# Tiled attentions of a decoder: row maxima in a ring of single banks, exponentials in halves, the maximum as a row of the query operand

## The reference, cut to what matters

```
scores = q_h @ k_h.T * scale            # 1024 x 1024 for each head
p      = softmax(scores, axis=-1)
out_h  = p @ v_h
y      = concat(out_h) @ Wo
```

## Time and profile before

| what | us |
|---|---|
| median of three runs | 2575.0 |
| the profiled execution, its own time | 2577.73 |
| its span | 2576.1 |
| TensorE matmul busy | 2238.0 (87%) |
| ScalarE busy | 1612.7 (63%) |
| VectorE busy | 985.3 (38%) |
| GpSimd busy | 453.3 (18%) |
| mean granted TensorE clock | 0.927 of 2.4 GHz |

### The profile page before, as it was taken

How to read it: one execution, slowest core, us unless ns; L and a number is a source line. 1 busy time by engine, 2 the same in 40 slices (tenths; PEclk the granted TensorE clock), 3 DMA queues, 4 the chain that set the end, 5 groups by cost and what they waited for, 6 DMA issues and landing times. The chain is left out here.

```text
span 2576.1 us, 30503 instructions
## 1 busy us (share of the span) xinstructions
PE 2238.0 (87%) x12294; PEld 741.9 (29%) x12294; DVE 985.3 (38%) x1557; ACT 1612.7 (63%) x1106; POOL 453.3 (18%) x202
## 2 busy tenths in 40 slices
PE   6999997689979858888799999999999847788797
PEld 2333332244446512222211111111111112222365
DVE  5667763154421366665211011011111146666111
ACT  1999899223322214444499999999999723444433
POOL 0577657200100004555200000000000000000000
PEclk9899999889989969888899999999999967888899
DMA  1000000226641030000100000100000000000010
GB/s 39 9 5 5 5 1 0 107 105 214 208 195 41 0 66 1 1 1 1 41 3 1 25 16 1 31 10 1 1 1 1 2 9 1 1 1 1 20 33 25
DMA packets 28990, 78.95 MB, mean 31 GB/s; under 512 B 3584, under 2 KB 18832, under 8 KB 26784
## 3 DMA queue, kind: packets, MB, share of 16 engines
q1 hardware_dynamic: 15032, 30.91, 4.1%
q0 software_dynamic: 4384, 29.56, 3.3%
q10 hardware_dynamic: 9448, 16.70, 1.8%
HBM read 71.61 MB, written 5.59 MB: 30 GB/s over the span
## 5 line engine op out<-in xcount | busy, mean ns | idle before, releaser
L1613 ACT ACTIVATE crat_E<-banks 128x1536 f32<-128x1536 f32 x544 | 749.4, 1461 | 20.7 <-PE banks L1513 6.8
L1529 PE MATMUL banks<-crat_E,crat_vst 128*32 128x512 f32 x3264 | 436.2, 607 | 0.2 <-ACT crat_E L1613 0.2
L1513 PE MATMUL banks<-crat_Q,mid_arena 52*128 52x512 bf16 x1632 | 329.3, 385 | 21.3 <-ACT crat_E L1613 17.1
L1640 DVE COPY crat_vst<-all_crossV 128x96 f32<-128x96 f32 x136 | 34.2, 252 | 640.7 <-PE banks L1529 640.6
L1276 ACT ACTIVATE rotat_E<-banks 128x2048 f32<-128x2048 f32 x64 | 120.1, 1877 | 178.0 <-PE banks L1167 178.0
L427 POOL TENSOR_TENSOR dist_wsum<-dist_wsum,dist_D 128x1024 f32<-128x1024 f32 x92 | 217.3, 2362 | 8.2
L1276 ACT ACTIVATE lastat_E<-banks 128x2048 f32<-128x2048 f32 x64 | 120.1, 1877 | 146.1 <-PE banks L1167 145.9
L1318 DVE TENSOR_REDUCE rotat_mx<-banks 128x1 f32<-128x512 f32 x256 | 164.9, 686 | 101.4 <-PE banks L1146 101.4
L1318 DVE TENSOR_REDUCE lastat_mx<-banks 128x1 f32<-128x512 f32 x256 | 164.8, 686 | 98.0 <-PE banks L1146 98.0
L345 DVE TENSOR_SCALAR dist_D<-banks,dist_k 128x512 f32<-128x512 f32 x256 | 178.6, 747 | 52.0 <-PE banks L213 52.0
L1513 PEld LDWEIGHTS banks<-crat_Q,mid_arena 52*128 52x128 bf16 x1632 | 60.1, 93 | 442.5 <-ACT crat_E L1613 317.1
(11 more groups left out here) (258 smaller groups left out, 2652.5 us busy)
## 6 DMA issues: line engine op xcount, KB each, us to landing
mlp_M<-in_mask POOLq DMA_DIRECT2D x28, 800.5 KB
mid_arena<-cross_k SPq DMA_DIRECT2D x42, 204.0 KB
moe_W<-in_experts SPq DMA_DIRECT2D x16, 512.0 KB, 3.6
mid_arena<-in_rot_tables ACTq DMA_DIRECT2D x8, 1024.0 KB, 18.1
mlp_C<-in_ctx SPq DMA_DIRECT2D x17, 384.0 KB, 4.4
cross_k<-mlp_kp ACTq DMA_DIRECT2D x17, 288.0 KB, 2.4
mlp_row<-in_mask POOLq DMA_DIRECT2D x1, 3202.0 KB, 12.9
mlp_M<-in_mask POOLq DMA_DIRECT2D x1, 3202.0 KB
```

The source lines that it names most:

```text
L1513: last = pe.matmul(PS[:, 3 * (at % 2) + k, :], K[s:s + ROWS, 2 * (g % 2) + pair, c * P:(c + 1) * P], Q[s:s + ROWS, 2 * g + pair, qh * HALF ...
L1529: last = pe.matmul(PS[32 * j:32 * j + 32, 6 + ps % 2, :], vst[:, (ps * STEPS + c // 3) % 3, c % 3, j, :], E[:, at // 3 % NE, at % 3, :], s ...
L1613: act.activation(flat(E[:, at % NE, :, :]), flat(PS[:, 3 * (at % 2):3 * (at % 2) + 3, :]), ACT.Exp, scale=CROSS_SCALE).then_inc(s_e, 1)
```

## The change

1. In `tiled_attention` a look is one matmul for one head into one bank. The two banks 4 and 5 are a ring: slot `i` waits for the reduce of slot `i - 2`, and the turn and the copy to `F` take a slot of their own. There are 32 looks a pass. They run further ahead: 5 a chunk in pass 0, 4 a chunk from then on, so that a pass's looks end two chunks before it; its turn is at the end of chunk 6 (pass 0: of chunk 7), and VectorE reduces 4 (or 8) looks of the pass after between the maxima and the row.
2. Each exponential is two activations of 128 x 1024. Scores of heads 0 and 1 wait for the first half of the chunk before, those of 2 and 3 for the second.
3. In the plain attention the ones products are gone. Each k tile has a row of ones in a free row of each head's 32, and the query operand `F` (f32 now, made by VectorE from `Q`, a mask and the turned maxima) holds minus the maximum in that row. `mb` is f32 with a copy for each group, its transposes are f32, and scores wait for `F`. The rotary attention keeps the three bf16 parts and the ones products.
4. `rotary_operands` adds on GpSimd and has two `A` buffers. `plain_operands` makes k's product a third time into banks 6 and 7, from which ScalarE casts with a mask as scale.

```diff
# rotary_operands
-                        if i:
-                            dve.wait_ge(s_sum, i)
-                        dve.tensor_tensor(A[:, eo, :], ...
+                        if i >= 2:
+                            dve.wait_ge(s_sum, i - 1)
+                        dve.tensor_tensor(A[:, i % 2, eo, :], ...
-                    dve.tensor_tensor(result(o), A[:, 0, :], A[:, 1, :], ALU.add).then_inc(s_sum, 1)
+                for i, o in enumerate(ORDER):
+                    pool.wait_ge(s_ta, 2 * i + 2)
+                    pool.tensor_tensor(result(o), A[:, i % 2, 0, :], A[:, i % 2, 1, :], ALU.add).then_inc(s_sum, 1)
# plain_operands
-                for o in range(2):
+                for o, at in ((0, 0), (1, 2), (1, 6)):
-                    act.wait_ge(s_k, j + 1)
-                    act.activation(Kb[:, j, :], K[:, j, :], ACT.Copy).then_inc(s_low, 1)
+                    act.activation(Kb[:, j, :], flat(PS[:, 6:8, :]), ACT.Copy, scale=rows[:, 0, j:j + 1]).then_inc(s_low, 1)
-                    dve.tensor_scalar(K[:, j, :], flat(PS[:, 2:4, :]), masks[:, j:j + 1], None, ALU.mult).then_inc(s_k, 1)
+                    dve.tensor_scalar(K[:, j, :], flat(PS[:, 2:4, :]), rows[:, 0, j:j + 1], rows[:, 1, j:j + 1], ALU.mult, ALU.add
# tiled_attention
-    SPREAD = [3, 2, 3, 2, 3, 2, 1, 0]
+    LOOKS = 4 * GROUPS * 2
+    def lag(ps):
+        return 0 if ps in (-1, 0, LAST) else 8 if ps == 1 else 4
+    def look_slot(ps, u):
+        return ps * (LOOKS + 1) + u - (u < lag(ps - 1))
+    def turn_slot(ps):
+        return (ps + 1) * (LOOKS + 1) - 1 + lag(ps)
+    def ahead(ps, c):
+        return min(5 * c if ps == 0 else 8 + LOOKS * ps + 4 * c, LOOKS * LAST)
+    def turned(ps):
+        return (ps - 1, NT - 1 if ps == 1 else NT - 2)
...
-                    pe.wait_ge(s_mt, ps * UNITS + u)
-                    for s in range(2):
-                        r = 32 * (2 * pp + s)
-                        last = pe.matmul(PS[:, MX + s, :], ...
+                def free(i):
+                    if i >= 2:
+                        pe.wait_ge(s_mt, i - 1)
+                    return MX + i % 2
+                    bank = free(look_slot(ps, u))
+                    pe.matmul(PS[:, bank, :], ...
...
                 def scores(ps, c):
-                    if at:
-                        pe.wait_ge(s_e, at)
+                    if c == 0 and not pairs:
+                        pe.wait_ge(s_mt, turn_slot(ps) + 1)
                     for r in range(4):
+                        if at and r % 2 == 0:
+                            pe.wait_ge(s_e, 2 * at - 1 + r // 2)
+                        of = half(Qs(g), ps % 2) if pairs else F[:, ps % 2, :]
+                        last = pe.matmul(PS[:, S + r, :], Ks(g)[32 * r:32 * r + 32, c * P:(c + 1) * P],
+                                         of[32 * r:32 * r + 32, :], start=True, stop=not pairs)
+                        if not pairs and r % 2:
+                            last.then_inc(s_s, 1)
+                    if pairs:
...
+                        for r in range(4):
+                            last = pe.matmul(PS[:, S + r, :], onesb[32 * r:32 * r + 3, :], F[32 * r:32 * r + 3, ps % 2, :],
+                                             start=False, stop=True)
+                            if r % 2:
+                                last.then_inc(s_s, 1)
...
-                    act.activation(flat(E[:, at % NE, :, :]), flat(PS[:, S:S + 4, :]), ACT.Exp, scale=scale).then_inc(s_e, 1)
+                    for i in range(2):
+                        act.wait_ge(s_s, 2 * at + i + 1)
+                        act.activation(flat(E[:, at % NE, 2 * i:2 * i + 2, :]), flat(PS[:, S + 2 * i:S + 2 * i + 2, :]), ACT.Exp,
...
+                for ps in range(PASSES):
+                    for u in range(lag(ps - 1), LOOKS):
+                        reduce(ps, u)
+                    maxima(ps)
+                    for u in range(lag(ps)):
+                        reduce(ps + 1, u)
+                    rows_of(ps)
```

More of the change, by code:

```diff
@@ L1211, in project @@
                         of.then_inc(s_y, 1)
-                pe.wait_ge(s_set, 3)
-                for u in range(UNITS):
-                    look(0, u)
+                pe.wait_ge(s_set, 3 if pairs else 2)
+                for at in range(LOOKS):
+                    look(at)
                 turn(0)
@@ L1219, in _ @@
                         scores(ps, c)
-                        units = range(AHEAD[c], AHEAD[c + 1]) if ps < LAST else range(0)
-                        for u in units[:(len(units) + 1) // 2]:
-                            look(ps + 1, u)
+                        first, end = LOOKS + ahead(ps, c), LOOKS + ahead(ps, c + 1)
+                        middle = (first + end + 1) // 2
+                        for at in range(first, middle):
+                            look(at)
                         if c:
@@ L1226, in _ @@
                             values(ps - 1, NT - 1)
-                        for u in units[(len(units) + 1) // 2:]:
-                            look(ps + 1, u)
+                        for at in range(middle, end):
+                            look(at)
                         if pairs and c == 1 and ps:
@@ L1285, in _ @@
             def _(pool):
-                pool.memset(mb.rearrange("q t w -> q (t w)"), 0.0).then_inc(s_set, 1)
+                of = mb.rearrange("q t w -> q (t w)") if pairs else mb.rearrange("q j t w -> q (j t w)")
+                pool.memset(of, 0.0).then_inc(s_set, 1)
                 def product(ps):
```

141 lines of the change are left out of this document (77 added, 64 removed).

## The result

The changed kernel takes 2487.8 us (four runs, 2483.57 to 2489.26) against 2575.5 for the kernel before (four runs on the same chip): a ratio of 0.9648, with a 95% interval of 0.9621 to 0.9675. Forecast were 2469, in a range of 2435 to 2520. So sign and range hold, and the time is 19 us above the forecast. The profiled execution's span is 2487.4 us, 88.7 less than before, where the terms of the forecast sum to 105.7: 17 us of the gain did not come. (The other 2 us lie in how far a profiled execution stands from the median before and after.)

What follows compares the result with a forecast made beforehand. No engine was full: looks and reduces took turns, and a chain through four score banks was the other limit. Terms summed to -105.7 us from 2577.7, so 2472.0, with the runs' median 2.7 lower: 2469, range 2435 to 2520.

Steps and rivals of the forecast that it cites:

- The forecast case: Whole kernel: the change works as worked out, -105.7 us in sum, to 2469 us; chance 0.68.
- the rotary passes: Rotary attention, passes 1 to 6: 32.5 us a pass against 37.7, -5.2 each, -31.2 in six.
- the passes 0: First pass of each attention: five looks a chunk and a low-clock start, 33 us, -4 each, -8 together.
- the plain passes: Plain attention, passes 1 to 6: chunks of 2.95 us, 27.6 us a pass against 35.9, -49.8 in six.
- with turn and maxima +1.3: Rotary passes 1 to 6: turn and maxima add 1.3 us a pass to chunks summing to 30.4.
- Initial looks: Ahead of each attention's first pass: 32 single looks in two banks take 22.4 us against 31.9, -9.5 each, -19.0.
- (A): Passes with looks: the clock dips stay at a mean of 0.87, +42 us, 2511 in total; chance 0.15.
- (B): Scores of a chunk: split pairs lose their fourfold overlap, 1.9 us instead of 0.96; total 2545; chance 0.08.
- (C): Look ring: no overlap, each look pays its whole round, 1.18 us at 2.4 GHz; total 2647; chance 0.02.
- (D): VectorE's reduces: with a wait between them they start 1.1 us apart; total 2590; chance 0.04.
- (E): Whole kernel: another in-order wait (row sums, the turn) takes up the gain, total within 0.5%; chance 0.03.
- the waits of looks: Sign in the profile: waits of looks on reduces fall from 157 and 144 us to under 50 each.

Runs made afterwards that it cites:

- e1: The changed kernel, with GpSimd's sum of chunks 4 and 5 waiting until VectorE's maxima steps are done: 2458.1 us, ratio 0.9518.
- e14: As e1, but four looks a chunk in pass 0 and five in pass 1, both turns after chunk 7, no GpSimd wait in pass 0: 2467.5 us.
- e3: The changed kernel with pass 0's looks dealt 6, 6, 5, 5, 5, 5, 4, 4 and pass 1's turn one chunk earlier: 2494.2 us, ratio 0.9659.
- e9: As e1, with two unread bf16 matmuls behind each of the last 16 initial looks, to fill TensorE ahead of pass 0: 2482.9 us, ratio 0.9627.

## Why the prediction came out as it did

**Sign and size.** The forecast case was the right one: ring and halves overlap, and the chunk is shorter. That the total is over it comes from two of its terms, the rotary passes and the passes 0, against a third, the plain passes.

**Rotary passes, -31.2 forecast, -14.3 measured: the step that failed.** The terms for the chunks were right in their sum (3.26 and 4.27 against 3.5 and 4.1, 7.53 and 7.6 together). What failed is "with turn and maxima +1.3": the maxima move two chunks ahead, and I costed them by their lengths before and not by what they would run beside at their new place. With GpSimd's sum of 4.53 us beside them their first step takes 3.65 us more, TensorE stands, and the clock drops. e1 takes the meeting away and a pass is 30.9, 1.6 better than the forecast's 32.5. The stall costs 28.0 us of six passes: 4.3 to 5.6 in each of passes 1 to 5 and 3.1 in pass 6. How much of it is the wait and how much the clock, 0.93 against 1.00, the runs don't separate. I wrote that GpSimd's pair sums are hidden because they take less than two chunks. That counts GpSimd's own time and overlooks who can't work beside it.

**Pass 0, -4 each forecast, +5.3 and -1.3 measured.** The term, five looks at the pace of VectorE with a low start, was too small: 33 us were a guess between the two, and 42.9 and 35.7 were measured. Chunks of five looks take 3.78 and 4.88 us at full clock (e14), the last one takes 8.18 and 7.13 with the turn at its end (5.32 and 2.81 in e3, without it), and the low level took more than I had given it: the clock is 0.50 over the first 11.0 us of the rotary pass 0 and 0.84 over the other 31.8, with a second low spell at its end. The place where the first spell ends varies between kernels that are alike up to there but for the row sums (passes of 42.8 and 47.4 us). What ends it stays open: two attempts to bring it about failed.

**Plain passes, -49.8 forecast, -59.2 measured.** Right in mechanism, too small in size. The chunk is 2.68 to 3.08 us against 2.95; the mean of the six chunks a pass without the spread and the turn is 2.85. The f32 turn takes 0.63 us for four tiles, and the chunk that holds it 4.81, 1.96 over the mean, where turn, maxima and row had 1.8. The chunk with the spread takes 4.38, 1.5 over it, where 1.4 was put. The 0.8 for a spell at the low level never came (clock 1.00). The pass is 26.3, not 27.6: 0.8 by the chunks and 0.8 by the clock, less 0.3 by these two.

**Initial looks and operands.** From the first look to the first exponential it is 27.3 us in the rotary and 27.4 in the plain attention against 36.4 in both, -9.1 and -9.0 for -9.5. Both starts came within 0.2 us of the terms (-8.2 for -8.4, -7.6 for -7.4), the plain one by some luck: what lies ahead of its looks grew by 1.5 us instead of 1.2, and what lies behind them by 0.1 instead of 0.9. The row sums on GpSimd cost the 1.1 us that they were given. The clock of the initial looks stayed at 0.50 as forecast, but the reason that I gave, an idle TensorE, is not in the rows: it is busy 21.7 of 27.4 us there, and all of 15.00 in e9. Pass 7 was 1.3 too high in the rotary attention and 1.2 too low in the plain one. The 1.9 us gained behind the last pass have no term and no experiment.

**Rivals.** (A), the dips stay: not in the plain attention (1.00). In the rotary one they are there (0.93), as a result of the stall; without it, in e1, they go. (B), scores lose their fourfold overlap: in part. In the plain attention the two pairs start up to 0.5 us apart and eight matmuls take 1.42 us in the median against 1.14, but they still overlap, and the chunk of 3.9 us that went with (B) did not come. (C), the ring doesn't overlap: no, four reduces in 2.61 us. (D), reduces 1.1 us apart: no, 0.64 to 0.70 with a wait ahead of each; the flush that the Trainium skill, "VectorE: DVE Perf Modes", section "The DRAIN you can't avoid", puts behind an operation does not show in these rows. (E): its mechanism, another wait in order that eats a gain, came true in one part, with GpSimd where I had looked only at TensorE's list. **What I said to look for** held for the 256 halves, both chunk lengths and the clock of the plain passes (1.00); the rotary passes stood at the bound I had named (0.93). It failed for the waits of looks, where I had taken idle time of the weight loads for idle time of TensorE.

## What to carry to other kernels

When a step moves to another place in the schedule, ask of its engine not only what waits behind it but what the other engines run at that very moment: a step of 0.2 us on VectorE that reads two SBUF inputs can wait out a GpSimd instruction of 4.5 us, and one wait on the side that isn't critical (GpSimd's) gives the time back. A short operation that is longer than its like in one place, as the 0.71 us step of before was, is worth a look at what ends 0.03 us ahead of it: such a wait stands in the length of the step itself, and no view of waits names it. Splitting the long instruction doesn't help if several such steps follow each other.
